# Bilinear sampling as one matmul over all pixels, with weights multiplied out and spread over partitions by DMA, in a new order of the last pass

## The chip, the cores and the metric

The kernel runs on one core of one Trainium2 chip. Its time is the device time of one execution in microseconds (us). The engines are PE (matmuls, with PEld for the loading of weights), DVE, ACT and POOL; SP issues the DMAs. Each runs its own program in order and they meet by semaphores.

## The reference

16 images of 16x16 pixels with 96 channels go through two layers. Layer 0 is a windowed attention and a binarized MLP whose activations are scaled by a maximum over groups of images. Layer 1, the last pass of the kernel, is a deformable attention and a mixture of experts. For every image it computes, in short:

```python
q = x @ w_q + b_q
t = gelu(layernorm(grouped_conv3x3(q)))          # 6 groups of 16 channels
offset = tanh(t_group @ w_offp) * (8, 8)         # one (y, x) per pixel and group
pos = offset + pixel
xs = bilinear_sample_zero(x_group, pos)          # zero outside the image
k, v = xs @ w_k, xs @ w_v
y = softmax(q k^T * scale) v @ w_o               # 12 heads, all 256 pixels
out = top2_of_4_experts(layernorm(x + y)) + ...
```

The bilinear sample of output pixel q in group g is the sum over all pixels (r, c) of hat(y_q - r) * hat(x_q - c) * x[r, c], where hat(d) = max(0, 1 - |d|).

## The kernel before, in words

The kernel has a setup, pass a (layer 0's attention), a short pass b and pass c (layer 1). Pass c is a software pipeline: in turn j, image j is in stage o (offsets), j-1 in s (sample), j-2 in k (split), j-3 in a (attend) and j-4 in e (experts) (BEHIND_C, L79). There are 4 turns that fill it, 12 in the loop and 4 that drain it. The string ORDER_C (L76) is the order of the work: each letter lets every engine run the next step of that stage, so all engines go through the letters in one and the same order, each at its own pace. Below, "o9" is the tenth letter o, and so on. Stages of different images are interleaved in this way and every engine still runs strictly in order: an instruction that waits holds all behind it on its engine.

Stage o: o0 scales the residual (ycl, L846) and SP loads xraw (L427), o1 adds them on DVE (L852, after waiting for xraw) and takes statistics, o2 normalizes (f_xn, L859), then come projection, 3x3 convolution, norm (L865 to L871) and Gelu; o9 is the offset matmul (PE, L1424) and ACT's tanh (L1152), o10 makes hat[group*16+r, axis, q] on DVE (L880 to L882).

How the weights get to the sampling: POOL splits f_xn and the vertical hat into three bf16 parts each (parts, L589 to L595, four operations a time). SP writes these to DRAM (L435, L447) and reads them back in another layout, six DMAs of 48 KB for rows (L444) and six for hatst (L452), so that a contraction over 96 partitions covers 16 rows times six products of parts. PE transposes the horizontal hat (L1429) and ACT copies it (hatx, L1156).

Stage s (L887, L1435) works on six pieces (two tiles of 128 pixels, three pairs of groups). PE contracts over rows (two bf16 matmuls, L1445) into PSUM bank 1, DVE multiplies by the horizontal weights (L896) and sums over columns (L899). One bank serves all pieces, so a piece of PE waits for DVE's multiplication of the piece before (L1443). Then PE transposes xs (L1450), ACT copies (L1166), PE makes keys and values (L1455).

Stage a: 24 transposes on PE (turn, L1470), copies on ACT (L1042), scores and their negated maxima on DVE (L920), then scores again, exponentials on ACT (L1198) and values on PE (L1499; four matmuls of 32 columns side by side, L1495). Stage e: projection, residual and norm (L942), gate, and four experts whose hidden parts share PSUM bank 6 (up L1557, down L1568).

SP is in order too. In each turn it issues the out DMA at e15 (L474), at o12 the reads of rows, the write and the reads of the hats, and at o0 of the next turn the load of xraw, which DVE needs at o1.

## Time and profile before

| | us |
|---|---|
| median of 3 runs | 1477.58 (1475.88 to 1477.93) |
| the profiled execution, its own time | 1476.25 |
| its span, first to last instruction | 1474.5 |
| pass c, first instruction to the end | 445.9 to 1474.5 |
| granted TensorE clock, mean | 0.76 |

Times in the trace count from the start of the span. "Idle before" is how long an engine had stood still before an instruction, and the arrow names what released it. The granted clock is a share of 2.4 GHz, so 0.50 is 1.2 GHz.

### The profile page before, as it was taken

Reading aid. Unit: us, or ns where it says so; the run is one execution under the profiler, and the core shown is the slowest. Engines: PE = TensorE matmul, PEld = TensorE weight load, DVE = VectorE, ACT = ScalarE, POOL = GpSimd, SP = SyncE. Lnnn points to the kernel's source line nnn. Section 1 sums busy time; section 2 is a strip of 40 time slices with the busy share of each in tenths; the row PEclk is TensorE's granted clock in tenths of the full one; section 3 lists DMA queues with packets and bytes.
Section 4 is the critical chain, followed back from the end, with each engine's and each line's share of the span. In section 5 each row is a group of like instructions: output and inputs, shape, how many; then the busy total and the mean of one; then the engine's idle time right before and its main releaser. Section 6 shows DMA issues by size and latency. Waiting matters only on the chain.

```text
span 1474.5 us, 26072 instructions
## 1 busy us (share of the span) xinstructions
PE 976.5 (66%) x8998; PEld 671.1 (46%) x8998; DVE 763.3 (52%) x2165; ACT 597.5 (41%) x1259; POOL 401.3 (27%) x525
## 2 busy tenths in 40 slices
PE   0266667666564434677777877767777878767876
PEld 0154555554343233354464563554544645534454
DVE  1156666555342444476465564564754655645342
ACT  0255556555351011433444425334334444254542
POOL 3377777776001021211111212111111112111000
PEclk9987676767585555787786886887877878878776
DMA  3000000000000100000000000000000000000000
GB/s 96 9 10 11 10 9 11 9 9 7 6 0 16 26 24 22 24 13 22 23 6 25 15 19 25 15 19 25 9 21 25 8 25 15 19 23 4 4 3 3
DMA packets 51853, 24.46 MB, mean 17 GB/s; under 512 B 37977, under 2 KB 49802, under 8 KB 51818
## 3 DMA queue, kind: packets, MB, share of 16 engines
q1 hardware_dynamic: 51818, 24.01, 6.5%
q8 instruction: 20, 0.33, 0.1%
q14 instruction: 15, 0.12, 0.0%
HBM read 16.10 MB, written 7.88 MB: 16 GB/s over the span
## 4 chain that ended last, share of the span: by engine, by line
PE 24%; issue 18%; DVE 11%; ACT 9%; POOL 3%; DMA 1%; DVEq 0%; SPq 0%; ACTq 0%; POOLq 0%
PE ps L1240 20%; ACT stackt L1042 3%; DVE nm L920 3%; DVE xs L899 2%; DVE samp L896 2%; ACT prob L1198 1%; PE ps L1245 1%; ACT L1198 1%; POOL srstd L516 1%; POOL hatr L592 1%; PE ps L1543 1%; DVE th L880 1%; DVE hat L881 1%; ACT th L1152 0%; ACT hb L1224 0%
## 5 line engine op out<-in xcount | busy, mean ns | idle before, releaser
L1042 ACT COPY stackt<-ps 128x768 bf16<-128x768 bf16 x192 | 142.8, 829 | 92.2 <-PE ps L1245 92.1
L1240 PE MATMUL ps<-stackt 53*64 53x64 bf16 (+3 forms) x2304 | 111.3, 247 | 87.5 <-ACT stackt L1042 50.6
L1240 PE MATMUL ps<-b_xnt,we 128*128 128x256 f32 x384 | 143.5, 494 | 2.6 <-ACT hb L1224 2.3
L1224 ACT ACTIVATE hb<-ps 128x512 f32<-128x512 f32 (+1 forms) x128 | 63.1, 493 | 202.3 <-PE ps L1240 202.1
L552 POOL TENSOR_TENSOR rn<-ss,neghalf 128x24 f32<-128x24 f32 x32 | 132.7, 4163 | 42.1 <-DVE ss L749 42.1
L920 DVE TENSOR_REDUCE nm<-ps 128x2 f32<-128x512 f32 x192 | 120.5, 685 | 30.1 <-PE ps L1240 26.9
L1198 ACT ACTIVATE prob<-ps 128x512 f32<-128x512 f32 x192 | 104.2, 594 | 63.9 <-PE ps L1240 63.8
L1240 PEld LDWEIGHTS ps<-stackt 53*64 53x64 bf16 (+3 forms) x2304 | 49.1, 115 | 170.8 <-issue 58.8
L516 POOL TENSOR_TENSOR prstd<-pveps,neghalf 128x2 f32<-128x2 f32 x48 | 42.5, 885 | 309.8 <-DVE pveps L709 302.5
L1240 PEld LDWEIGHTS ps<-we,hb 128*128 128x128 f32 x768 | 110.7, 220 | 26.0 <-ACT hb L1224 20.5
L1240 PE MATMUL ps<-we,hb 128*128 128x96 f32 x768 | 111.8, 303 | 15.8 <-ACT hb L1224 15.8
L1240 PE MATMUL ps<-prob,va 64*32 64x64 f32 (+1 forms) x2304 | 110.4, 366 | 3.9 <-ACT prob L1198 3.9
L896 DVE TENSOR_TENSOR samp<-ps,hatx 128x512 f32<-128x512 f32 x96 | 66.1, 689 | 84.5 <-PE ps L1240 82.1
L1245 PE MATMUL ps<-identb,stack 128*128 128x128 bf16 x1152 | 98.4, 253 | 9.6 <-DVE stack L726 6.0
L899 DVE TENSOR_REDUCE xs<-samp 128x32 f32<-128x512 f32 x96 | 97.6, 1016 | 3.3
L1245 PEld LDWEIGHTS ps<-identb,stack 128*128 128x128 bf16 x1152 | 89.6, 117 | 19.8 <-DVE stack L726 9.7
L1240 PE MATMUL ps<-wconv,qpad 128*128 128x96 f32 x576 | 80.0, 300 | 21.5 <-ACT y1all L1140 21.5
L1240 PE MATMUL ps<-rows,hatst 128*128 128x256 bf16 x192 | 50.1, 356 | 65.8 <-DVE samp L896 45.2
L1240 PEld LDWEIGHTS ps<-b_xnt,we 128*128 128x128 f32 x384 | 81.9, 244 | 17.3 <-ACT hb L1224 6.0
L1240 PEld LDWEIGHTS ps<-wconv,qpad 128*128 128x128 f32 x576 | 77.9, 216 | 24.7 <-ACT qpad L1139 23.9
L516 POOL TENSOR_TENSOR srstd<-sveps,neghalf 128x2 f32<-128x2 f32 x32 | 22.3, 696 | 153.6 <-DVE sveps L709 153.6
L591 POOL CAST hatp<-hat 96x256 bf16<-96x256 f32 x16 | 6.3, 397 | 208.5 <-DVE hat L882 167.8
(229 smaller groups left out, 1676.4 us busy)
## 6 DMA issues: line engine op xcount, KB each, us to landing
rows<-xn_scratch SPq DMA_DIRECT2D x96, 48.0 KB, 1.9
hatst<-hat_scratch SPq DMA_DIRECT2D x96, 48.0 KB, 2.1
xn_scratch<-xnp SPq DMA_DIRECT2D x48, 48.0 KB, 1.8
hat_scratch<-hatp SPq DMA_DIRECT2D x16, 144.0 KB, 1.9
xraw<-x_scratch SPq DMA_DIRECT2D x16, 96.0 KB, 2.0
out<-acc SPq DMA_DIRECT2D x16, 96.0 KB, 1.8
we<-in_we SPq DMA_DIRECT2D x1, 768.0 KB
xin<-in_x SPq DMA_DIRECT2D x16, 48.0 KB, 1.8
```

The source lines that it names most:

```text
L516: g.tensor_tensor(n["rstd"][:], n["veps"][:], neghalf[:, 0:TILES], ALU.pow).then_inc(S(ready), 1)
L552: g.tensor_tensor(rn[:, t].rearrange("p a h -> p (a h)"), ss[:, t, :], neghalf[:, 0:2 * HEADS], ALU.pow).then_inc(S("a_rn"), 1)
L592: own.link(g.tensor_tensor(left, src, part(0), ALU.subtract))
L880: own.link(v.scalar_tensor_tensor(flat(th), flat(th), SIDE / 2.0, flat(posc), ALU.mult, ALU.add))
L896: v.tensor_tensor(samp[:, k % 2], ps[:, 1, :].rearrange("p (a c) -> p a c", c=GC), hx.to_broadcast([P, 2 * SIDE, GC]), ALU.mult).then_inc( ...
L899: ins = v.tensor_reduce(xs[:, t, 2 * GC * b:2 * GC * (b + 1)].rearrange("p (g k) -> p g k", g=2), samp[:, k % 2].rearrange("p (g c) k -> p ...
L920: v.tensor_reduce(nm[:, t, a, 2 * pq:2 * pq + 2], ps[:, score_bank(u // 2) + a, :].rearrange("p (b n) -> p b n", n=TOK), AX.X, ALU.max, ne ...
L1042: return a.copy(stackt[:, x, :, P * t:P * t + P], bank_bf(bank))
L1198: a.activation(prob[:, u % 4].rearrange("p b n -> p (b n)"), ps[:, 4 + u % 2, :], ACT.Exp, scale=float(HD) ** -0.5).then_inc(S("c_exp"), 1)
L1224: a.activation(hb[:, e % 2].rearrange("p m n -> p (m n)")[:, 2 * TOK * k:2 * TOK * k + n_], ps[:, 6, 0:n_], ACT.Gelu).then_inc(S("c_h"), 1)
L1240: return m.matmul(o, l, r, start=start, stop=stop)
L1245: ins = m.transpose(bank_bf(bank)[:, b, :], stack[:, x, t].rearrange("p h c -> p (h c)")[:, P * b:P * b + P], identb[:])
```

## The change

The split in bf16 parts, the DMAs of rows, the transposes of the horizontal hat and of xs, DVE's six multiplications and six sums and PSUM's intermediate result go. Instead the sampling is one contraction over all 256 pixels, with one weight for each pixel and output. hat is written to DRAM in f32 by two DMAs and read back by three: hatx puts the horizontal hat of column p mod 16 on partition p (16 rows of 6144 bytes, repeated 8 times), haty[t] the vertical hat of row 8t + p div 16 (8 rows, each repeated 16 times). These are 768 KB each. DVE multiplies haty by hatx for four of the groups, POOL for two. PE then runs twelve f32 matmuls (two tiles, six groups) with 32 stationary columns from xz, a copy of f_xn by POOL with the other group of a pair left zero; the result is already transposed. ORDER_C is a new string of 54 letters, s has 6 steps instead of 8. In the new order o0 and o1 come first in a turn, before e0; s0 (first multiplications) is the eighth letter; o9 is at the place of the 42nd and o10 at that of the 49th. The matmuls of s stand at s3 and s4.

```diff
-ORDER_C = "eeeoeeosaeaasaseeeoaaeeeaooseoeaokokkeaeassaasooaaoasoao"
+ORDER_C = "ooeeaoeseeaaoeaaeeeoaaeeeoeaoekoeasosseaaoaksaakoaaoos"
...
-        hatx = sb("hatx", [P, TILES, DG, SIDE])
-
-        xnr = sb("xnr", [P, TILES, C])
-        xnp = sb("xnp", [P, 3, TILES, C], BF16)
-        hatr = sb("hatr", [C, TOK])
-        hatp = sb("hatp", [C, 3, TOK], BF16)
-        rows = sb("rows", [P, SIDE, C], BF16)
-        hatst = sb("hatst", [P, DG, TOK], BF16)
-        samp = sb("samp", [P, 2, 2 * SIDE, GC])
-        xs = sb("xs", [P, TILES, C])
+
+        xz = sb("xz", [P, TILES, DG // 2, 2, 2 * GC])
+        haty = sb("haty", [P, TILES, DG, TOK])
+        hatx = sb("hatx", [P, DG, TOK])
...
-        xn_dram = nc.dram_tensor("xn_scratch", [3, TOK, C], BF16).ap()
-        hat_dram = nc.dram_tensor("hat_scratch", [C, 3, TOK], BF16).ap()
+        hat_dram = nc.dram_tensor("hat_scratch", [2, SIDE, DG, TOK], F32).ap()
...
-                w("rows_in", 0)
+                for _ in range(ORDER_C.count("o") - 3):
+                    yield
+                w("hat", 1)
                 settle(sp, "sp")
-                w("xnp", 1)
+                for axis in range(2):
+                    sp.dma_start(hat_dram[axis].rearrange("r g q -> g r q"), hat[:, axis, :]).then_inc(S("c_hat_out"), 16)
+                w("xst", 0)
                 settle(sp, "sp")
-                for k in range(3):
-                    sp.dma_start(xn_dram[k].rearrange("(t p) c -> p t c", p=P), xnp[:, k, :, :]).then_inc(S("c_xn_out"), 16)
-                for _ in range(ORDER_C.count("o") - 3):
-                    yield
-                w("t3", 0)
+                w("hat_out", 32)
                 settle(sp, "sp")
-                w("xn_out", 48)
-                settle(sp, "sp")
-                for slot in range(6):
-                    src = xn_dram[ROW_PARTS[slot]].rearrange("(r c) k -> r c k", c=SIDE)
-                    sp.dma_start(rows[SIDE * slot:SIDE * slot + SIDE, :, :], src).then_inc(S("c_rows_in"), 16)
-                w("hatp", 1)
-                settle(sp, "sp")
-                sp.dma_start(hat_dram, hatp[:, :, :]).then_inc(S("c_hat_out"), 16)
-                w("hat_out", 16)
-                settle(sp, "sp")
-                for slot in range(6):
-                    src = hat_dram[:, HAT_PARTS[slot], :].rearrange("(g r) q -> r g q", r=SIDE)
-                    sp.dma_start(hatst[SIDE * slot:SIDE * slot + SIDE, :, :], src).then_inc(S("c_hat_in"), 16)
+                row = DG * TOK
+                src = bass.AP(hat_dram.tensor, hat_dram.offset + SIDE * row, [[0, SIDE // 2], [row, SIDE], [1, row]])
+                sp.dma_start(hatx[:].rearrange("p g q -> p (g q)"), src).then_inc(S("c_hat_in"), 16)
+                for t in range(TILES):
+                    src = bass.AP(hat_dram.tensor, hat_dram.offset + t * (SIDE // 2) * row, [[row, SIDE // 2], [0, SIDE], [1, row]])
+                    sp.dma_start(haty[:, t].rearrange("p g q -> p (g q)"), src).then_inc(S("c_hat_in"), 16)
...
-            def parts(own, src, left, part, ready):
-
-                own.link(g.tensor_copy(part(0), src))
-                own.link(g.tensor_tensor(left, src, part(0), ALU.subtract))
-                yield
-                own.link(g.tensor_copy(part(1), left))
-                g.tensor_tensor(part(2), left, part(1), ALU.subtract).then_inc(ready, 1)
+            def weights(g_):
+                return haty[:, :, g_, :], hatx[:, g_:g_ + 1, :].to_broadcast([P, TILES, TOK])
...
-                w("xn_out", 0)
-                w("xn", 1)
-                settle(pool, "pool")
-                yield from parts(own, f_xn[:], xnr[:], lambda k: xnp[:, k], S("c_xnp"))
...
-                w("hat_out", 0)
-                w("hat", 1)
+                w("xst", 0)
+                w("xn", 1)
                 settle(pool, "pool")
-                yield from parts(own, hat[:, 0, :], hatr[:], lambda k: hatp[:, k, :], S("c_hatp"))
+                for odd in range(2):
+                    ins = g.tensor_copy(xz[:, :, :, odd, GC * odd:GC * odd + GC],
+                                        f_xn[:].rearrange("p t (b a k) -> p t b a k", a=2, k=GC)[:, :, :, odd, :])
+                ins.then_inc(S("c_xz"), 1)
+                yield
                 yield
 
             def sample_c(i):
-                for _ in range(8):
+                w = waits(pool, "c_", i)
+                w("hat_in", 48)
+                for g_ in (1, 3):
+                    y, x = weights(g_)
+                    g.tensor_tensor(y, y, x, ALU.mult).then_inc(S("c_pmul"), 1)
+                    yield
+                for _ in range(ORDER_C.count("s") - 2):
...
-                w("hatp", 0)
-                w("hxt", 0)
+                w("hat_out", 0)
...
             def sample_c(i):
                 w = waits(dve, "c_", i)
-                own = Own(dve, "dve_sample")
-                for k in range(6):
-                    t, b = k // 3, k % 3
-                    if k == 0:
-                        w("hatx", 1)
-                    w("t3", k + 1)
-                    hx = hatx[:, t, 2 * b:2 * b + 2, :].rearrange("p g c -> p (g c)")
-                    v.tensor_tensor(samp[:, k % 2], ps[:, 1, :].rearrange("p (a c) -> p a c", c=GC),
-                                    hx.to_broadcast([P, 2 * SIDE, GC]), ALU.mult).then_inc(S("c_mul"), 1)
-                    w("mul", k + 1)
-                    ins = v.tensor_reduce(xs[:, t, 2 * GC * b:2 * GC * (b + 1)].rearrange("p (g k) -> p g k", g=2),
-                                          samp[:, k % 2].rearrange("p (g c) k -> p g k c", g=2), AX.X, ALU.add)
-                    if k == 5:
-                        ins.then_inc(S("c_xs"), 1)
-                    else:
-                        own.link(ins)
-                    yield
-                yield
-                yield
+                w("hat_in", 48)
+                for g in (0, 2, 4, 5):
+                    x = hatx[:, g:g + 1, :].to_broadcast([P, TILES, TOK])
+                    v.tensor_tensor(haty[:, :, g, :], haty[:, :, g, :], x, ALU.mult).then_inc(S("c_mul"), 1)
+                    yield
+                for _ in range(ORDER_C.count("s") - 4):
...
-                w("mul", 0)
-                w("hxt", 1)
-                a.copy(hatx[:].rearrange("p t g c -> p (t g c)"), ps[:, 0, 0:2 * C]).then_inc(S("c_hatx"), 1)
...
-                w("hat", 1)
-                for t in range(TILES):
-                    ins = m.transpose(tiles(0, C)[:, t, :], hat[:, 1, cols(t)], ident[0:C, 0:C])
-                ins.then_inc(S("c_hxt"), 1)
...
                 w = waits(pe, "c_", i)
+                yield
+                yield
+                yield
                 w("v", 0)
-                w("rows_in", 96)
-                w("hat_in", 96)
-                for k in range(6):
-                    t, b = k // 3, k % 3
-                    if k >= 1:
-                        w("mul", k)
-                    for g in (2 * b, 2 * b + 1):
-                        ins = mm(ps[:, 1, TOK * (g % 2):TOK * (g % 2) + TOK], hatst[:, g, cols(t)], rows[:, :, GC * g:GC * g + GC])
-                    ins.then_inc(S("c_t3"), 1)
-                    yield
-                w("xs", 1)
-                for t in range(TILES):
-                    ins = m.transpose(ps[0:C, 1, cols(t)], xs[:, t, :], ident[:])
+                w("xz", 1)
+                for odd in range(2):
+                    w("mul", (3, 4)[odd])
+                    if odd:
+                        w("pmul", 2)
+                    settle(pe, "pe")
+                    for t in range(TILES):
+                        for b in range(DG // 2):
+                            ins = mm(ps[32 * b:32 * b + 32, 1, 0:TOK], xz[:, t, b, odd, :], haty[:, t, 2 * b + odd, :],
+                                     t == 0 and odd == 0, t == TILES - 1 and odd == 1)
+                    if odd == 0:
+                        yield
                 ins.then_inc(S("c_xst"), 1)
```

## Rows read from the trace of the kernel before

**Rows 1.** The page, part 1: busy time of each engine, share of the span, instructions.
```profile
PE 976.5 (66%) x8998; PEld 671.1 (46%) x8998; DVE 763.3 (52%) x2165; ACT 597.5 (41%) x1259; POOL 401.3 (27%) x525
```
**Rows 2.** Start of L880 (us, duration) in the first and last of 13 turns, timeline of DVE.
```profile
610.60 0.69 DVE L880 SCALAR_TENSOR_TENSOR th<-th,posc 96x512 f32<-96x512 f32 x1 [4.36 <-ACT th L1152]
...
1306.69 0.69 DVE L880 SCALAR_TENSOR_TENSOR th<-th,posc 96x512 f32<-96x512 f32 x1 [5.35 <-ACT th L1152]
```
**Rows 3.** Windows of a turn: length, busy PE, PEld, DVE, ACT, POOL, clock, DMA, GB/s.
```profile
918.90:955.30 36.40, 27.54 (x204) 19.69 (x204) 24.00 (x53) 13.65 (x30) 6.08 (x12) 0.87 0.06 15
955.30:976.20 20.90, 14.90 (x94) 8.87 (x94) 9.68 (x38) 10.04 (x21) 3.80 (x7) 0.74 0.09 26
```
**Rows 4.** Groups by line and shape in the turn 910.5 to 967.8: busy us, mean ns.
```profile
L899 DVE TENSOR_REDUCE xs<-samp 128x32 f32<-128x512 f32 x6 | 6.1, 1020 | 0.2
L1240 PE MATMUL ps<-prob,va 128*32 128x256 f32 x48 | 5.1, 512 | 0.3 <-ACT prob L1198 0.3
...
L896 DVE TENSOR_TENSOR samp<-ps,hatx 128x512 f32<-128x512 f32 x6 | 4.1, 688 | 4.0 <-PE ps L1240 3.8
...
L1240 PE MATMUL ps<-rows,hatst 128*128 128x256 bf16 x12 | 2.8, 322 | 2.2 <-DVE samp L896 2.2
...
L1450 PE MATMUL ps<-ident,xs 128*96 128x128 f32 x2 | 0.7, 436 | 0.0
```
**Rows 5.** Waits in the same turn: engine and line, releaser, us in total, times, longest.
```profile
PE ps L1240 <- DVE samp L896: 2.2, 2, 1.4
...
PE ps L1394 <- DVE f_xn L714: 1.5, 1, 1.5
...
PE ps L1240 <- ACT y1all L1140: 1.3, 1, 1.3
```
**Rows 6.** Timeline from the offset matmul to the next turn: start us, us, engine, line.
```profile
955.32 2.02 PE L1240 MATMUL ps<-tnt,woffp 128*96 128x256 f32 x4 [0.46 <-ACT tnt L1149]
...
959.55 0.42 DVE L882 TENSOR_SCALAR hat<-hat 96x512 f32<-96x512 f32 x1
...
962.57 0.30 SPq L447 DMA_DIRECT2D hat_scratch<-hatp  x1
...
964.51 2.67 SPq L452 DMA_DIRECT2D hatst<-hat_scratch  x6
...
965.51 0.35 DVE L942 TENSOR_TENSOR xres<-y1all,ps 128x192 f32<-128x192 f32 x1 [1.88 <-PE ps L1240]
...
967.61 0.57 DVE L714 TENSOR_SCALAR b_xn<-xres,smv,srstd 128x96 f32<-128x96 f32 x2 [0.80 <-POOL srstd L516]
...
970.23 2.05 PE L1240 MATMUL ps<-b_xnt,we 128*128 128x256 f32 x4
...
972.03 0.35 DVE L852 TENSOR_TENSOR xin<-xraw,ps 128x192 f32<-128x192 f32 x1 [0.23 <-DVE sc L958]
...
973.69 0.69 POOL L516 TENSOR_TENSOR prstd<-pveps,neghalf 128x2 f32<-128x2 f32 x1 [6.11 <-DVE pveps L709]
```
**Rows 7.** Windows in the setup: large loads in rows of some KB; eight ebraw loads.
```profile
16.00:18.00 2.00, 0.00 (x0) 0.00 (x0) 0.00 (x0) 0.00 (x0) 0.00 (x0) 1.00 0.99 356
...
32.00:33.00 1.00, 0.00 (x0) 0.00 (x0) 0.00 (x0) 0.00 (x0) 0.00 (x0) 1.00 0.63 73
```
**Rows 8.** DMA packets while bt_scratch is written, ebraw is read, hat_scratch is written.
```profile
DMA packets 24, 0.01 MB, mean 8 GB/s; under 512 B 12, under 2 KB 24, under 8 KB 24
...
DMA packets 832, 0.35 MB, mean 55 GB/s; under 512 B 832, under 2 KB 832, under 8 KB 832
...
DMA packets 112, 0.15 MB, mean 134 GB/s; under 512 B 16, under 2 KB 112, under 8 KB 112
```
**Rows 9.** Timeline of DVE, first to second turn: hat done, then xraw used.
```profile
475.25 0.42 DVE L882 TENSOR_SCALAR hat<-hat 96x512 f32<-96x512 f32 x1
...
485.05 0.35 DVE L852 TENSOR_TENSOR xin<-xraw,ps 128x192 f32<-128x192 f32 x1 [8.68 <-DMA xraw<-x_scratch]
```
**Rows 10.** Durations (ns min/median/max) of one DVE line with two inputs in SBUF.
```profile
L871 DVE TENSOR_TENSOR tn<-tn,lnb x16: 357/958/964, 469.1 to 1291.4; 128x192 f32<-128x192 f32 x16
```

More of the change, by code:

```diff
@@ L257, in build_program @@
         gam_ready = [plain_sem(f"gamma_ready{n}") for n in range(2)]
-        own_sems = {k: plain_sem(k) for k in ("dve_first", "dve_mid", "dve_last", "dve_sample", "pool_split", "pool_parts")}
+        own_sems = {k: plain_sem(k) for k in ("dve_first", "dve_mid", "dve_last", "dve_sample", "pool_split")}
         signals("a_", "sp", x_in=48, x1_out=48)
@@ L270, in build_program @@
         signals("b_", "pe", y2=GIMG)
-        signals("c_", "sp", x_in=16, xn_out=48, rows_in=96, hat_out=16, hat_in=96, out=16)
-        signals("c_", "dve", ycl=1, xadd=1, var=1, xn=1, cvar=1, cn=1, hat=1, mul=6, xs=1, nm=12, parts=1,
+        signals("c_", "sp", x_in=16, hat_out=32, hat_in=48, out=16)
+        signals("c_", "dve", ycl=1, xadd=1, var=1, xn=1, cvar=1, cn=1, hat=1, mul=4, nm=12, parts=1,
                 on=2, x3=1, var3=1, xn3=1, gsub=1, acc=2)
-        signals("c_", "pool", rstd=1, xnp=1, crstd=1, hatp=1, va=1, split=1, rstd3=1)
-        signals("c_", "act", xnt=1, qpad=1, q_new=1, cg=1, tnt=1, tanh=1, hatx=1, xst_sb=1, k_sb=1, v=1,
+        signals("c_", "pool", rstd=1, crstd=1, xz=1, pmul=2, va=1, split=1, rstd3=1)
+        signals("c_", "act", xnt=1, qpad=1, q_new=1, cg=1, tnt=1, tanh=1, xst_sb=1, k_sb=1, v=1,
                 copies=1, qt_sb=2, kt_sb=2, q2t_sb=2, exp=12, ot=3, ont=1, x3t_sb=1, gexp=1, h=8)
-        signals("c_", "pe", yt=1, xt=1, qc=1, q=1, conv=1, tt=1, offs=1, hxt=1, t3=6, xst=1, kv=1,
+        signals("c_", "pe", yt=1, xt=1, qc=1, q=1, conv=1, tt=1, offs=1, xst=1, kv=1,
                 qt=2, kt=2, s=12, q2t=2, st=12, pv=12, otr=2, ontp=1, proj=1, x3t=1, gate=1, h1=8, y=2)
@@ L358, in build_program @@
         DSETUP = 28
-        PZERO = 16
+        PZERO = 15
         PSETUP = PZERO + 6
@@ L497, in _ @@
                 setup(g.memset(t[:], 0.0))
-            setup(g.memset(rows[:], 0.0))
-            setup(g.memset(hatst[:], 0.0))
+            setup(g.memset(xz[:], 0.0))
             setup(g.memset(bias3[:], 0.0))
@@ L587, in _ @@
             pool.wait_ge(setup_pool, PSETUP + 1)
-            def parts(own, src, left, part, ready):
-                own.link(g.tensor_copy(part(0), src))
-                own.link(g.tensor_tensor(left, src, part(0), ALU.subtract))
-                yield
-                own.link(g.tensor_copy(part(1), left))
-                g.tensor_tensor(part(2), left, part(1), ALU.subtract).then_inc(ready, 1)
+            def weights(g_):
+                return haty[:, :, g_, :], hatx[:, g_:g_ + 1, :].to_broadcast([P, TILES, TOK])
             def offsets_c(i):
                 w = waits(pool, "c_", i)
-                own = Own(pool, "pool_parts")
                 yield
@@ L1162, in sample_c @@
                 w = waits(act, "c_", i)
-                for _ in range(6):
+                for _ in range(ORDER_C.count("s") - 2):
                     yield
@@ L1384, in offsets_c @@
                 w = waits(pe, "c_", i)
-                w("hatx", 0)
+                w("tanh", 0)
                 w("ycl", 1)
```

4 lines of the change are left out of this document (1 added, 3 removed).

## The prediction

> **What bounds the kernel now.** I read the page first: PE is busy 66% of the span and no engine more [rows 1], so the end is set by chains, not by one engine's work. The change touches pass c alone, so I look at its turn. The offsets' first DVE step (L880) starts at 610.60 and twelve turns later at 1306.69 [rows 2]: 58.0 us a turn. The turn whose timeline I use takes 57.3, and I cut it where PE starts the scores and where it starts the offset matmul. The middle, 36.4 us, has PE busy 27.5 and DVE 24.0 at a clock of 0.87; the wrap around the turn's end, 20.9 us, has PE busy only 14.9 at 0.74 [rows 3]. In the middle PE stands still 8.9 us. The waits of the turn say for whom: 2.2 us for DVE's multiplication of the samples, 1.5 for f_xn, which DVE reaches only after sample work, 1.3 for ACT's copies before the convolution [rows 5]. In the wrap the chain runs offset matmul, tanh, hat (done at 959.97), out and back through DRAM, and beside it projection, norm and gate [rows 6].
>
> **What goes.** DVE loses six pairs of 0.688 and 1.020 us, 10.2 us a turn. PE loses twelve matmuls (2.8) and two transposes of xs (0.7) [rows 4]. Ten of the twelve (2.3) and the transposes stand in the middle. POOL loses eight operations of the split, which no PE instruction waited for directly. SP loses 16 DMAs and keeps 5 beside xraw and out.
>
> **What comes.** Four multiplications of 128x512 f32 on DVE; the old ones, with one input in PSUM, took 0.688 [rows 4], so 2.8 us, and DVE's net is -7.4. With both inputs in SBUF a line can be held up: L871 takes 357 ns alone and 958 in most turns, when POOL works beside it [rows 10]. The bounds for one multiplication are 0.69 and about 1.9 (that ratio); I take 0.7 to 1.2, because only two multiplications of POOL stand beside the four. The nearest row for the twelve new matmuls is prob,va: 48 records, two for each f32 matmul, busy 5.1 us with strips of 32 columns side by side [rows 4], so 0.21 each and 2.6 for twelve. If strips did not overlap, a record's 512 ns would give up to 12 us; three strips instead of four make 3.5. I take 2.6, half of it in the middle, for it is the same shape on the same engine.
>
> The Trainium skill (SBUF — State Buffer, Who interferes with whom) says that a DVE instruction with two SBUF inputs and a GpSimd instruction that reads SBUF exclude each other. By it a multiplication of DVE could wait for a whole one of POOL. The trace agrees in kind (357 against 958 ns).
>
> **The middle, added up.** PE work: 27.5 - 2.3 - 0.7 + 1.3. The new order also moves one of six score and value steps (0.85 of values, with its scores an estimated 1.5) and f_xn's transposes (0.4) to the wrap, and an expert step (estimated 0.6) in. That gives 24.5. Of the 8.9 idle I take off 5.0: no sample wait, f_xn made long before its use, and expert and score steps between ACT's copies and the convolution. The middle becomes 24.5 + 3.9 = 28.4, a gain of 8.0. What is late next there is the pace of scores, exponentials and maxima.
>
> **The wrap, added up.** Here the change adds the wait that I think decides. SP issues three loads of 768 KB and then, in the same queue, xraw of the next image; o1 on DVE waits for xraw, and o1 now stands ahead of e0. Behind it on DVE wait the residual and norm of e1 and f_xn; POOL's power and PE's gate wait for these.
> From the start of the offset matmul: hat is done after 4.65 us (955.32 to 959.97). The store: the second issue starts 0.5 later, and from the issue of the old store to the next DMA's issue 1.94 went by (962.57 to 964.51) [rows 6]; with 0.5 more because the new store's outermost dimension is six groups (see the packets below), 3.0 us. Then 1.3 us until data flow and land, an estimate from the same 1.94. Then 2.36 MB. The full rate in this trace is 356 GB/s at a busy share of 0.99 [rows 7], which gives 6.6 us. But the packet counts tell something else: a store from 12 partitions has 12 packets beside its 12 rows, the eight ebraw loads of 96 rows each have 832 - 768 = 64, eight apiece, and the hat store from 96 partitions has 112 - 96 = 16 [rows 8]. The extra packets follow the outermost dimension, and are at most 16; I read them as one per DMA engine that takes part. Those loads of eight outermost rows moved only 73 GB/s [rows 7]. The three new loads all have eight outermost in their source (8 repeats, or 8 rows), so I expect half the engines: 2.36 MB at 178 GB/s is 13.2 us; eight engines alone may be a little quicker each, and I take 12.5. xraw lands at hat + 3.0 + 1.3 + 12.5 = 16.8. The bounds of this term are 6.6 and, at ebraw's rate, 32.
> After xraw: the addition and statistics, 1.7 (972.03 to 973.69); the residual's norm to b_xn, 2.7 (965.51 to 968.18); then transposes, gate and first expert step, 4.1 (968.18 to 972.28) [rows 6]; less 0.1 that overlaps: 8.4. The wrap is 4.65 + 16.8 + 8.4 = 29.85, against 20.9 before. Of PE's work there, some 14.4 us need no xraw (14.9, less an estimated 3.7 of gate and experts, plus 1.9 and 1.3 that the order puts there), with some 3 of waits for exponentials; then it stands still for some 7 us.
>
> The Trainium skill (DMA: Bandwidth & Descriptors, Why a DMA increments its semaphore by 16 and not by 1) speaks against this change: a DMA from SP uses the largest number of engines up to 16 that divides the slowest dimension of both sides, and the lowest-numbered ones. By it the three loads queue on the same eight engines, one behind the other, and the store runs on six. The packet counts agree with the number; which engines they are, no row here shows.
>
> **The sum.** A loop turn: 28.4 + 29.85 = 58.25, +0.95 against 57.3; twelve make +11.4. In turns 2 and 3 xraw came 9.4 us after hat (475.67 to 485.05) [rows 9] and DVE stood 8.7 for it; now 16.8, so +7.4, less about 3 for sampling that leaves f_xn's way: +4.4 each, and +1.5 for turn 4. Turn 17, without offsets: -3 for the sampling, +3 for late weights. Turns 18 to 20 hold attention and experts alone: 0, the same steps in about the same interleaving. Setup: nothing, one memset less on POOL under the loads. Sum: 1476.25 + 11.4 + 10.3 = 1498.0. The profiled execution is 1.3 below the median of the runs, so no correction is worth making.
>
> **Rivals.** A: all 16 engines take part. The extra packets might count something else, and ebraw's rows are short and badly placed. Then xraw is at hat + 10.9, the wrap 4.65 + 10.9 + 8.4 = 23.95, a turn 52.35: -4.95 x 12 = -59, the first turns -2, turn 17 -4: 1411, faster. It decides at PE's own work in the wrap: as long as xraw comes within 12 to 13 us of hat, the middle's gain of 8 us stays. B: eight engines a load, but not the same eight, so that loads overlap: 8.7 us of data, a turn of 54.5, 1476 - 34 + 1 = 1443. C: a repeated read of the same 6 KB rows is slow. At ebraw's 73 GB/s the data take 32 us, 19.5 more in each of 16 turns: 1810. For it speaks only that no load of before repeats rows; against it, that ebraw's rows are 452 bytes and these 6144. D: the change is neutral because wrap and middle trade exactly; that lies inside the forecast's own error, 1 us a turn being 16 us.
> The forecast itself has +-2 us a turn (DVE's multiplications up to 1.2, strips of PE, idle of 3.9 between 2 and 6), so 1465 to 1535.
>
> **Chances.** Forecast 0.62 (a tenth of it ends faster, a tenth the same), A 0.20, B 0.12, C 0.06. A measurement here tells 0.2% (3 us) from no change. Faster: 0.20 + 0.12 + 0.06 = 0.38; same 0.06; slower 0.56. The range must reach down to A, 1410, and up to the forecast's 1535; left out are C and half of A.
>
> **What would show it.** DMA share in the wrap near 0.5 for 12 us with about 180 GB/s; DVE's L852 idle for 5 to 10 us before it, released by xraw; sixteen or eight extra packets for each of the three loads; the middle down to 28 or 29 us; PE idle for 5 to 8 us before f_xn's transposes, and the clock at 1.2 GHz there. I am wrong if xraw lands less than 13 us after hat, or if the middle stays at 36 us.

## The result, and the profile after

The changed kernel takes 1644.3 us (median of 4 runs, 1639.6 to 1647.5) beside 1477.3 for the kernel before (4 runs): a ratio of 1.113 [1.110, 1.116]. The forecast was 1498, with a range from 1410 to 1535. The direction was right and the size was not.

The page of the changed kernel, parts 1, 4, 5 and 6, in lines that answer to [rows 1] or are new:

```profile
PE 913.2 (56%) x9126; PEld 645.0 (39%) x9126; DVE 673.7 (41%) x2037; ACT 588.9 (36%) x1243; POOL 409.3 (25%) x460
...
issue 52%; PE 18%; POOL 9%; DVE 8%; DMA 6%; ACT 4%; SPq 2%; POOLq 1%; DVEq 0%; ACTq 0%
...
L836 DVE TENSOR_TENSOR xin<-xraw,ps 128x192 f32<-128x192 f32 x16 | 5.7, 354 | 340.4 <-DMA xraw<-x_scratch 340.4
...
L875 DVE TENSOR_TENSOR haty<-haty,hatx 128x512 f32<-128x512 f32 x64 | 65.3, 1058 | 18.2 <-DMA haty<-hat_scratch 18.2
...
xraw<-x_scratch SPq DMA_DIRECT2D x16, 96.0 KB, 21.1
```

PE is 63 us less busy than before, DVE 90, and the span is 163 longer. The one new large number is the third line: DVE's o1, the addition of the residual (L836), stands idle for 340 us in 16 turns, and what ends it is the load of xraw, a transfer of 96 KB that needs 21.1 us from issue to landing. The waits by engine show who stands behind DVE:

```profile
PE ps L1362 <- DVE f_xn L698: 357.5, 16, 30.3
ACT f_xnt L1103 <- PE ps L1362: 352.3, 16, 34.3
DVE xin L836 <- DMA xraw<-x_scratch: 340.4, 16, 27.2
```

One wait passes through three engines. Now the timeline of one loop turn, which answers to [rows 6] (start us, us, engine, line):

```profile
1260.31 1.10 PE L1208 MATMUL ps<-tnt,woffp 128*96 128x256 f32 x4
...
1263.59 0.42 DVE L865 TENSOR_SCALAR hat<-hat 96x512 f32<-96x512 f32 x1
1264.12 1.56 SPq L426 DMA_DIRECT2D hat_scratch<-hat  x2
1268.12 0.61 SPq L433 DMA_DIRECT2D hatx<-hat_scratch  x1
1268.78 1.22 SPq L436 DMA_DIRECT2D haty<-hat_scratch  x2
1270.62 0.41 SPq L418 DMA_DIRECT2D xraw<-x_scratch  x1
1292.03 0.35 DVE L836 TENSOR_TENSOR xin<-xraw,ps 128x192 f32<-128x192 f32 x1 [22.09 <-DMA xraw<-x_scratch]
...
1295.79 0.66 PE L1362 MATMUL ps<-ident,f_xn 128*96 128x128 f32 x2 [22.70 <-DVE f_xn L698]
...
1295.95 1.54 DVE L698 TENSOR_SCALAR b_xn<-xres,smv,srstd 128x96 f32<-128x96 f32 x2 [0.22 <-POOL srstd L499]
1296.17 1.26 POOL L604 TENSOR_TENSOR haty<-haty,hatx 128x512 f32<-128x512 f32 x1
...
1297.55 0.67 PE L1509 MATMUL ps<-ident,b_xn 128*96 128x128 f32 x2 [1.10 <-DVE b_xn L698]
...
1299.55 2.05 PE L1208 MATMUL ps<-b_xnt,we 128*128 128x256 f32 x4
```

SP's queue works first in, first out here: xraw is issued 0.6 us after the last haty and lands behind all 2.36 MB. And the windows of the same turn, with the columns of [rows 3]:

```profile
1260.31:1301.54 41.23, 13.70 (x120) 7.98 (x116) 9.57 (x33) 11.31 (x24) 3.65 (x6) 0.69 0.29 65
1301.54:1329.43 27.89, 25.13 (x193) 18.54 (x192) 18.80 (x50) 12.38 (x28) 6.97 (x9) 0.87 0.01 4
1270.00:1292.00 22.00, 2.63 (x32) 2.20 (x32) 0.00 (x0) 3.27 (x5) 0.00 (x0) 0.63 0.49 109
```

The first window is the wrap, the second the middle. The middle fell from 36.4 to 27.9 us, as the change could hope; the wrap grew from 20.9 to 41.2. In the third window PE and ACT finish what they have (2.63 and 3.27 us busy, all before 1275.2); from there to the landing of xraw only DMA works. The window has half of the 16 DMA engines busy, at 109 GB/s. Over the span, by the start of ACT's tanh: from the first to the fourth, in the fill, 171.9 us against 136.8 before (+35); the 12 turns from there 68.8 us each against 58.0 (+130); from the last tanh to the end 168 in both. That is the 163 us of the spans, the rest lying before the first tanh.

### The profile page after: what moved, and what is told of

Same layout as the page of the kernel before. It is cut to its first block, busy times and chain, and to the rows that moved or that the text cites. A ratio compares the mean times of both kernels' runs of the same rounds, so it can differ in the third digit from the quotient of the medians.

```text
span 1637.8 us, 25699 instructions
## 1 busy us (share of the span) xinstructions
PE 913.2 (56%) x9126; PEld 645.0 (39%) x9126; DVE 673.7 (41%) x2037; ACT 588.9 (36%) x1243; POOL 409.3 (25%) x460
## 3 DMA queue, kind: packets, MB, share of 16 engines
q1 hardware_dynamic: 32938, 50.73, 13.5%
## 4 chain that ended last, share of the span: by engine, by line
issue 52%; PE 18%; POOL 9%; DVE 8%; DMA 6%; ACT 4%; SPq 2%; POOLq 1%; DVEq 0%; ACTq 0%
PE ps L1208 17%; POOL rn L535 3%; DMA xraw<-x_scratch 3%; POOL prstd L499 2%; DVE haty L875 2%; DMA haty<-hat_scratch 1%; POOL haty L604 1%; ACT prob L1166 1%; POOL va L506 1%; SPq L358 1%; POOL srstd L499 1%; DVE tn L698 1%; PE ps L1329 1%; DMA hat_scratch<-hat 1%; ACT sq L1025 1%
## 5 line engine op out<-in xcount | busy, mean ns | idle before, releaser
L1362 PE MATMUL ps<-ident,f_xn 128*96 128x128 f32 x32 | 10.6, 435 | 357.5 <-DVE f_xn L698 357.5
L1208 PE MATMUL ps<-b_xnt,we 128*128 128x256 f32 x384 | 134.3, 466 | 25.9 <-ACT hb L1192 25.7
L836 DVE TENSOR_TENSOR xin<-xraw,ps 128x192 f32<-128x192 f32 x16 | 5.7, 354 | 340.4 <-DMA xraw<-x_scratch 340.4
L891 DVE TENSOR_REDUCE nm<-ps 128x2 f32<-128x512 f32 x192 | 119.2, 683 | 44.8 <-PE ps L1208 43.8
L1103 ACT COPY f_xnt<-ps 96x256 f32<-96x256 f32 x16 | 5.9, 367 | 352.3 <-PE ps L1362 352.3
L1208 PEld LDWEIGHTS ps<-we,hb 128*128 128x128 f32 x768 | 105.5, 212 | 13.1 <-issue 8.8
L1208 PE MATMUL ps<-prob,va 64*32 64x64 f32 (+1 forms) x2304 | 90.5, 327 | 9.2 <-ACT prob L1166 9.2
L1208 PEld LDWEIGHTS ps<-b_xnt,we 128*128 128x128 f32 x384 | 75.0, 225 | 43.9 <-ACT hb L1192 35.4
L1213 PE MATMUL ps<-identb,stack 128*128 128x128 bf16 x1152 | 87.9, 237 | 7.8 <-DVE stack L710 4.5
L1213 PEld LDWEIGHTS ps<-identb,stack 128*128 128x128 bf16 x1152 | 79.0, 108 | 17.8 <-DVE stack L710 8.2
L875 DVE TENSOR_TENSOR haty<-haty,hatx 128x512 f32<-128x512 f32 x64 | 65.3, 1058 | 18.2 <-DMA haty<-hat_scratch 18.2
## 6 DMA issues: line engine op xcount, KB each, us to landing
xraw<-x_scratch SPq DMA_DIRECT2D x16, 96.0 KB, 21.1
```

Of the source, the lines that this page charges most:

```text
L875: v.tensor_tensor(haty[:, :, g, :], haty[:, :, g, :], x, ALU.mult).then_inc(S("c_mul"), 1)
L891: v.tensor_reduce(nm[:, t, a, 2 * pq:2 * pq + 2], ps[:, score_bank(u // 2) + a, :].rearrange("p (b n) -> p b n", n=TOK), AX.X, ALU.max, ne ...
L1208: return m.matmul(o, l, r, start=start, stop=stop)
L1213: ins = m.transpose(bank_bf(bank)[:, b, :], stack[:, x, t].rearrange("p h c -> p (h c)")[:, P * b:P * b + P], identb[:])
```

## The experiments

My theory after the result: the 2.36 MB move far slower than the engines' full rate, and what they cost is the wait of o1 for xraw behind them. Rivals: rows read again and again are slow; the number of engines alone is the cause; or the new order is at fault. Each kernel was run once with a profile, beside the kernel before (1471 to 1476 us), unless a number of runs is given. The kernels that read another tensor, and lanes16, leave out the right sampling weights; they are there for their times alone. A packet time is the median over the packets of 6144 B of the first exchange in the loop's fill, where nothing else runs.

### The transfer: how many engines, and which rows

**distinct8.** The same eight engines, but 128 different rows of another tensor.

```diff
-src = AP(hat_dram, ..., [[0, 8], [row, 16], [1, row]])            # hatx; haty alike
+src = AP(we1, ..., [[row, 8], [row * 8, 16], [1, row]])           # both
```

> The three loads of 768 KB read 128 different rows of 6144 bytes (those of an input of weights) instead of 16 or 8 rows repeated; still eight outermost, same count and size of packets, same destination. The weights of the sampling are other numbers, so the output is another. Theory P (eight engines, and each slowed at the SBUF side because several write neighbouring partitions together): packets stay at 455 ns, 115 GB/s, time 1640 +-10. Theory R (repeated reads of the same rows are slow): packets near 234 to 270 ns, xraw some 10 us earlier a turn, time near 1480.

Measured 1613.5 us; L836 waits 312 us, a packet takes about 400 ns instead of 455, and xraw lands after 19.4 us. Repetition costs at most 31 of 1644 us. The other theory did not come out exactly either: it expected packets to stay at 455 ns.

**lanes16.** The two outer dimensions of each source exchanged, so 16 groups of 8.

```diff
-[[0, 8], [row, 16], [1, row]]     # hatx
+[[row, 16], [0, 8], [1, row]]
-[[row, 8], [0, 16], [1, row]]     # haty
+[[0, 16], [row, 8], [1, row]]
```

> The two outer dimensions of each source are exchanged, so that 16 stand outermost: hatx [16 rows, each 8 times], haty [16 times, 8 rows]. Same rows, same bytes; partition p gets the row of another pixel, so the output is another. Theory R: the same 115 GB/s or so, DMA share near 1 or packets of 900 ns, time 1640. Theory E (only the number of engines matters): 2.36 MB at 350 GB/s or near, xraw at hat + 12 instead of 28, PE's own work ends the wrap, time near 1410 to 1430. Theory P: 16 engines, each with 8 neighbouring partitions, somewhere from 216 to 350 GB/s, time 1410 to 1490.

Measured 1473.9 us, 58.8 us a turn. L836 waits 182 us, xraw lands after 10.5. All 16 engines work, yet a packet takes 444 ns, as slow as with eight. So 230 GB/s, not 356.

**distinct16.** Sixteen groups, different rows.

```diff
+src = AP(we1, ..., [[row, 16], [row * 16, 8], [1, row]])          # both
```

> Like lanes16 (16 outermost, all engines), but the loads read 128 different rows instead of repeated ones; the weights of the sampling are other numbers, so the output is another. So far a packet of 6144 bytes took 455 ns (8 engines, repeated), 400 (8, distinct), 444 (16, repeated), against 234 for the load of weights in the setup. Theory P (what slows each engine is where it writes: the source's three-dimensional form gives each engine a block of neighbouring partitions): 400 to 440 ns, 230 to 260 GB/s, time 1455 to 1475. Theory R (repetition slows at 16 engines): packets near 240 ns, 350 GB/s, time 1425.

Measured 1473.4 us, 439 ns a packet, L836 waits 184 us: repeated rows play no part with 16 engines.

**flat16.** The plain form: row p to partition p.

```diff
+src = we1.rearrange("p e h -> p (e h)")                           # both
```

> The three loads read the weights' array in its plain form, 128 rows onto 128 partitions, as the load in the setup does; same bytes, packets and destination, 16 engines; the sampling's weights are other numbers, so the output is another. Theory P: packets back to about 234 ns and 350 GB/s, because here the engines write partitions apart from each other: xraw at hat + 12.5, time 1420 to 1435. Rival (pass c's own traffic or the row size slows an engine, whatever the form): 400 ns as in the others, time 1455 to 1475.

Measured 1404.5 us, below the 1420 to 1435 expected, 53.8 us a turn, 234 ns a packet, L836 waits 117 us. Here are the windows of the first exchange, first of distinct16 (last columns: clock, DMA share, GB/s):

```profile
482.00:484.00 2.00, 0.00 (x0) 0.00 (x0) 0.00 (x0) 0.00 (x0) 0.00 (x0) 0.50 0.99 221
484.00:486.00 2.00, 0.00 (x0) 0.00 (x0) 0.00 (x0) 0.00 (x0) 0.00 (x0) 0.50 1.02 224
```

The same windows of flat16:

```profile
482.00:484.00 2.00, 0.00 (x0) 0.00 (x0) 0.00 (x0) 0.00 (x0) 0.00 (x0) 0.50 1.02 412
484.00:486.00 2.00, 0.00 (x0) 0.00 (x0) 0.00 (x0) 0.00 (x0) 0.00 (x0) 0.50 0.99 412
```

All 16 engines are busy in both; the bytes differ by 1.85. And of the changed kernel:

```profile
485.00:490.00 5.00, 0.00 (x0) 0.00 (x0) 0.00 (x0) 0.00 (x0) 0.00 (x0) 0.50 0.52 117
```

Half the engines, each at the slow rate of distinct16 and not at that of flat16. Two factors of nearly two stand on top of each other.

### What makes a packet slow

**block16.** flat16's rows and addresses, written as 16 groups of 8.

```diff
+src = AP(we1, ..., [[row * 8, 16], [row, 8], [1, row]])           # both
```

> Each of the three large transfers reads the 128 rows of we1 as flat16 does, row p to partition p, but written as 16 groups of 8 rows instead of 128 rows, so the weights hold other numbers. If the source's addresses made the packets of distinct16 slow (its rows were read in another order), packets take about 235 ns here and the run is flat16's 1404 us. If the form does it (16 groups, each engine with one run of 8 neighbouring partitions), packets take about 440 ns and the run is distinct16's 1473 us.

Measured 1402.2 us and 234 ns. The rule "three dimensions are slow" fell, unless these dimensions are merged into one of 128 on the way, which the trace doesn't tell.

**split16.** Each load becomes eight plain ones of 16 partitions with the right rows, 24 in all.

```diff
+for r in range(8):
+    sp.dma_start(hatx[16 * r:16 * r + 16], AP(hat_dram, 16 * row, [[row, 16], [1, row]]))
+for t in range(2):
+    for r in range(8):
+        sp.dma_start(haty[16 * r:16 * r + 16, t], AP(hat_dram, (8 * t + r) * row, [[0, 16], [1, row]]))
```

> The three transfers are issued as 24 plain ones of 16 partitions each, with the same rows to the same partitions, so each engine should get one partition of each 16. Theory (an engine is slow where it writes a run of neighbouring partitions): packets near 235 ns although haty's source row is the same 16 times. Rival (reading the same row again, or the store's rows just written, slows them): packets stay at 400 ns or more. In both cases the issues bind: SP needed 0.66 us from hatx's issue to haty's, so 24 take about 16 us and xraw lands some 18 to 20 us after the first, not much before the 22 of the changed kernel: 1560 to 1640 us.

Measured 1551.8 us, and 682 ns a packet, for hatx's different rows and for haty's repeated ones alike. My theory of neighbouring partitions for one engine is refuted: here each engine writes partitions 16 apart and is slower than ever. The 24 issues took 11.0 us, not 16. Two explanations were left: neighbouring source rows read at the same time, or partitions written at the same time.

**blockgap16.** block16, its groups 512 bytes nearer in the source, so that nothing can be merged.

```diff
-[[row * 8, 16], [row, 8], [1, row]]
+[[row * 8 - 128, 16], [row, 8], [1, row]]
```

> block16 with the groups 512 bytes nearer each other in the source, so that it cannot be merged into one run of 128 rows; the weights hold other numbers. At any moment 16 engines read rows 48 KB apart. Theory (ways into SBUF: in the order of lanes16, engines 8 partitions apart write at once and two share a way): packets 415 to 465 ns, run about 1473 us, like distinct16. Rival (neighbouring source rows): 234 ns and 1403 us, like block16.

Measured 1479.8 us and 423 ns; in the second half of the exchange, groups of 32 packets alternate between about 405 and 441 ns. Far source rows don't help.

**splitfar16.** split16's 24 loads, with source rows 48 KB apart.

```diff
+src = AP(we1, r * row, [[row * 8, 16], [1, row]])                 # both
```

> split16 with source rows of we1 that lie 48 KB apart (eight rows) in each of the 24 transfers of 16 neighbouring partitions; the weights hold other numbers. Theory (ways into SBUF): packets stay at 680 to 715 ns, the run at about 1550 us. Rival (neighbouring or repeated source rows): packets near 234 ns, the issues (4.0 and 7.7 us by split16's trace) bind and the run is 1450 to 1490 us.

Measured 1558.4 us and 691 ns. Windows of the first exchange, splitfar16:

```profile
480.00:485.00 5.00, 0.00 (x0) 0.00 (x0) 0.00 (x0) 0.00 (x0) 0.00 (x0) 0.50 1.04 144
485.00:490.00 5.00, 0.00 (x0) 0.00 (x0) 0.00 (x0) 0.00 (x0) 0.00 (x0) 0.50 1.02 140
```

The same of split16:

```profile
480.00:485.00 5.00, 0.00 (x0) 0.00 (x0) 0.00 (x0) 0.00 (x0) 0.00 (x0) 0.50 1.06 149
485.00:490.00 5.00, 0.00 (x0) 0.00 (x0) 0.00 (x0) 0.00 (x0) 0.00 (x0) 0.50 1.04 144
```

With 16 engines, changing the source to other rows or to rows far apart changes little in either arrangement (423 to 444 ns, and 682 to 691); with eight engines it took 455 to 400. So repeated, neighbouring or far rows don't explain 234 against 440 or 690 ns, and how the destination partitions are divided over the engines is what is left. That is an argument by exclusion, with two gaps. block16 must be counted as the plain form. And both fast forms read 768 KB that lie in one piece, while no run loads 128 partitions in the plain form from scattered rows; against a source in one piece as the cause speaks only that each of split16's hatx loads reads one piece of 96 KB and is slow. Which partitions meet is inferred too, since the packet records name no engine:

| engines and the partitions that they write at one time, if the outermost dimension is dealt to them in equal runs | packet, ns |
|---|---|
| flat16, block16: plain 128 | 234 |
| lanes16, distinct16, blockgap16: 16 engines, 8 apart | 423 to 444 |
| changed kernel: 8 engines, 16 apart | 455 |
| split16, splitfar16: 16 engines, neighbours | 682 to 691 |

The Trainium skill (SBUF — State Buffer, Door 1: The DMA port swizzle) has a map that fits: 16 ports of 8 partitions, where four neighbours share one with the four that lie 32 further. By it the second and third line put two engines on each port in use and the last one four. The plain transfer has one port per engine (the Trainium skill, DMA: Bandwidth & Descriptors, The descriptor swizzle). An estimate from flat16's 234 ns would be 468 ns with two on a port and 936 with four. The first is 3 to 11% above the 423 to 455 measured, so the traces agree roughly. The second is above the 682 to 691 measured; successive transfers of split16 fall on different ports by that map, so engines that drift apart would meet less, but no run here shows that.

### The wait, and the order

**xraw_act.** The load of xraw from ACT's queue, at o0.

```diff
-sp.dma_start(xraw[...], x1_dram[...]).then_inc(S("c_x_in"), 16)    # SP, turn's start
+act.dma_start(xraw[...], x1_dram[...]).then_inc(S("c_x_in"), 16)   # ACT, o0
```

> ACT issues the load of xraw, so it doesn't queue behind the weights; nothing else changes. My theory (the wait of o1 for xraw holds the projection's norm and f_xn): L836 waits under 3 us, but DVE and POOL now wait at s0 (eighth letter) for the weights, some 12 to 15 us; 4 to 6 us a turn gained, time near 1560. Rival (the weights' lateness alone sets the turn, through s0): no gain, 1630 to 1645.

Measured 1507.5 us, 60.7 a turn: a larger gain than expected, and not in the way expected. L836 still waits 175 us, not under 3 a turn, and xraw takes 13.7 to land instead of 21.1: from another queue it does not get past engines that are full, it only shares them. And a new wait stands behind, DVE's for haty, 109 us.

**old_order.** The changed kernel's sampling with ORDER_C of before (and s on DVE, POOL and PE delayed by two more empty steps).

> The new sampling with ORDER_C of the kernel before (two more empty steps of s in front, so that the first multiplications stand at the third s). o1 now stands behind e0 to e4. Theory (the wrap's wait is the loss, and the old order overlaps the norm, gate and first expert step, 6.8 us, with it): about 6 us a turn gained, time near 1550. Rival (the new order is worth more in the middle than it costs in the wrap): 1640 or more.

Measured 1635.2 us, 67.1 a turn, 272 us of waits for xraw. The expected 6 us a turn did not come, only 1.7, and no run here shows what held the rest. So the new order is not the cause of the loss, but gives nothing either as long as the wait stands.

**early8.** xraw is loaded one turn ahead: after o1's addition SP issues the load of the next image (x1_scratch gets one image more, so that the last turn loads something).

```diff
 # SP, pass c, at o2
+w("xadd", 1)
+sp.dma_start(xraw[:, :, :], x1_dram[i * TOK:(i + 1) * TOK])
```

> The load of xraw for the next image is issued by SP in the same turn, right after o1 has read the buffer, long before the weights' loads; the loads stay as in the changed kernel (eight engines). L836 no longer waits for a DMA. But s0, eighth letter, waits for the weights, which land 28 us after hat: the turn ends about 3.7 + 27.5 + 2 + 28 = 61 us long. Time 1490 to 1530, near the run with xraw on ACT (1507). Rival (xraw was the only wait that matters): 1350 to 1400.

Measured 1523.4 us, 61.9 a turn. The wait for xraw is gone, and most of it has come back elsewhere. Waits of early8:

```profile
DVE haty L877 <- DMA haty<-hat_scratch: 274.0, 16, 23.5
```

340 us for xraw became 274 for haty: s0 stands early in the order, before e0.

**early8_late** puts s0 behind o5, **late8** does that without the early xraw:

```diff
-ORDER_C = "ooeeaoeseeaaoeaaeeeoaaeeeoeaoekoeasosseaaoaksaakoaaoos"
+ORDER_C = "ooeeaoeeeaaoeaaeeeoaaeeeoseaoekoeaosseaaoaksaakoaaoos"
```

> As early8, and the letter s0 (first multiplications on DVE and POOL) moved from the eighth place to behind o5, so nothing waits for the weights in the wrap although they still take 28 us on eight engines. Theory (the loss is two waits for the transfer, and the transfer itself costs nothing once it is covered): no DMA wait above 1 us on DVE and POOL in the loop, turn 49 to 51 us, time 1340 to 1380, below the kernel before. Rival (three f32 multiplications in a row, f32 matmuls or the new order limit the middle): turn above 55 us, time above 1430.

> The changed kernel with one letter moved: s0 from the eighth place to behind o5. The load of xraw stays behind the weights' loads. If o1's wait for xraw is the only wait that sets the wrap in the changed kernel: no change, 1630 to 1645, L836 still waits 21 us a turn. Rival (the first multiplications in the wrap cost something of their own): 10 us or more faster.

Measured: early8_late 1333.1 us, 47.8 a turn; late8 1648.6, the changed kernel's time. Neither wait may be first in line: with both out of the way the transfer, still 115 GB/s, costs little in the loop (perm16_late, below, has it faster and its 12 turns are 7 us shorter). Waits of early8_late:

```profile
POOL haty L606 <- DMA haty<-hat_scratch: 285.3, 16, 23.9
...
DVE haty L877 <- DMA haty<-hat_scratch: 65.4, 8, 23.3
```

POOL's 285 us are harmless as far as the waits show: DVE waits for POOL's normalizing steps no longer than in the changed kernel (f_xn 15.3 against 14.6 us, b_xn 23.6 against 23.3). DVE's 65 are nearly all in the first three exchanges (22.9, 23.3, 13.8 us), in the fill, where no other work covers them.

**old_early.** The old order with xraw early; the first multiplications stand one step later than in old_order, at the fourth s.

> The new sampling in the order of the kernel before (first multiplications at the fourth s), with xraw loaded early, so no DMA wait is left in the loop, as in the fastest run. It divides that run's gain of 139 us between the sampling and the order. If the sampling alone gives it (10 us of DVE a turn gone): 1340 to 1370. If the new order gives part: 1380 to 1430. I expect 1400, because in the old order PE still waits for the norm of e1 behind other work.

Measured 1404.7 us. This parts the change: without the wait for xraw the new sampling gives 70 us in the old order, and the new order, with s0 late, another 72 (1333.1). The load of xraw behind the weights and s0 ahead of them take 311 together (1644.3 - 1333.1): with xraw alone put right 190 are left (early8).

### Faster versions

**perm16_late.** early8_late with lanes16's sources. To keep the sum right, the pixels of a tile lie on the partitions as (c r) instead of (r c): xraw and out move in two DMAs each, the copies of f_xnt and ont read permuted.

> As early8_late, but the pixels of a tile lie on the partitions by column first, so that the loads of the weights have 16 outermost and run on all 16 engines; xraw is loaded and the output stored in two DMAs each, and three copies read or write with a stride. The weights arrive 10 us earlier. Theory (a covered transfer costs nothing): within 10 us of early8_late's 1333. Rival (late weights or DMA traffic still hold something there): 1310 or less.

Measured 1287.7 us, 45 below early8_late, where at most 10 were expected. The first three exchanges of the fill, uncovered, make 31 of it (126.3 against 95.0 us from the first tanh to the fourth; waits for haty 59.9 against 29.7), the loop 7, the drain 10. "Covered" was true of the loop only.

**final.** early8_late with the second s moved forward too.

```diff
-ORDER_C = "ooeeaoeeeaaoeaaeeeoaaeeeoseaoekoeasosseaaoaksaakoaaoos"
+ORDER_C = "ooeeaoeeeaaoeaaeeeoaaeeeosesaoekoeaosseaaoaksaakoaaoos"
```

> As early8_late, with the letter s1 (second multiplications) moved forward to behind e9 as well, so that DVE's multiplications no longer stand three in a row, beside POOL's, ahead of PE's matmuls, where PE waits 1.8 us for them. Theory: 0.5 to 1.5 us a turn, time 1310 to 1327. Rival (the scores' maxima on DVE are then late instead): 1333 or more. Either way more than 9% under the kernel before.

Measured 1305.2 us (5 runs), ratio to before 0.885 [0.884, 0.887]; 45.3 us a turn, 2.5 less than early8_late where 0.5 to 1.5 was expected.

**split16_final** and **perm16_final**: final with split16's loads, and with perm16_late's pixels.

> split16's transfers in the version of the label final (xraw early, sampling late). If packets are fast, the last haty lands about 17 to 19 us after the first issue instead of 22 to 24, so the waits of the three filling turns (60 us in all) shrink by about 4 us each and the loop keeps its 45.3 us a turn: 1285 to 1305 us, against 1305. If SP, now busy some 16 us longer with issues at o1, delays the load of xraw at o2, then nothing is lost, since that load has a turn of slack.

> perm16_late with the order of final. Between perm16_late and early8_late the trace puts 31 of the 45 us in the first three turns after the fill (126.3 us against 95.0 from the first tanh to the fourth, waits for haty 59.9 against 29.7), where nothing covers the exchange, and 7 in the loop and 10 in the drain. If that is the cause, it adds to final's gain of 2.5 us a turn in the loop: final's 1305 less 31 to 45, 1260 to 1274 us. If the gain of the pixel order lay in the loop's cover, final's tighter loop would change it and the sum is off by over 10 us.

Measured 1250.8 us (4 runs), 0.850 [0.847, 0.854], and 1251.3 us (4 runs), 0.850 [0.847, 0.853]: 15% below the kernel before and 24% below the changed one, and not to be told apart. Both came out below what was expected. They come to the same time by different ways: the fill, first tanh to fourth, takes 111.9 us in split16_final and 96.5 in perm16_final, the twelve turns 512.4 and 525.1. In split16_final a turn is 42.7 us instead of final's 45.3, and the timeline shows a part of it. A turn of final:

```profile
901.95 2.94 POOL L606 TENSOR_TENSOR haty<-haty,hatx 128x512 f32<-128x512 f32 x2 [16.49 <-DMA haty<-hat_scratch]
902.25 3.19 DVE L877 TENSOR_TENSOR haty<-haty,hatx 128x512 f32<-128x512 f32 x2
```

A turn of split16_final:

```profile
864.45 2.49 POOL L608 TENSOR_TENSOR haty<-haty,hatx 128x512 f32<-128x512 f32 x2 [10.69 <-DMA haty<-hat_scratch]
870.49 1.29 DVE L879 TENSOR_TENSOR haty<-haty,hatx 128x512 f32<-128x512 f32 x2
```

The weights land some 6 us earlier against the tanh, POOL has done its half before DVE comes to its own, and DVE's two take 1.29 us instead of 3.19. This turn of final is one of the worse: over its twelve turns the two take 2.0 to 3.5 us, 2.6 on average, in split16_final always 1.29. That is 1.3 of the 2.6 us a turn, if it is all on DVE's path, which no run isolates. The granted clock also rose, from 0.93 to 0.96 over the twelve turns. The page of perm16_final, parts 1 and 4:

```profile
PE 866.9 (70%) x9126; PEld 615.7 (50%) x9126; DVE 671.4 (54%) x2037; ACT 590.2 (47%) x1243; POOL 404.6 (33%) x460
...
issue 27%; PE 20%; DMA 19%; POOL 12%; DVE 11%; ACT 6%; SPq 4%; POOLq 0%; DVEq 0%; ACTq 0%
```

"issue" is down from 52% to 27% of the chain, and PE does the same 9126 matmuls in 46 us less, its clock being granted at 0.84 on average instead of 0.75.

## Why the prediction was right and wrong

The turn from 1260.31 to 1329.43 takes 69.1 us; 58.25 were forecast. Term by term:

| term | forecast | measured |
|---|---|---|
| offset matmul to hat done | 4.65 | 3.70 |
| hat done to the first load's issue (store and back) | 3.0 | 4.1 |
| from there to the use of xraw | 1.3 + 12.5 | 23.9 |
| use of xraw to the first score matmul | 8.4 | 9.5 |
| middle | 28.4 | 27.9 |

**The step that failed** is the third: "2.36 MB at 178 GB/s is 13.2 us; eight engines alone may be a little quicker each, and I take 12.5". The number of engines was right, the rate of one was not: 356 GB/s by 16 engines was taken as 22 GB/s for any engine in any transfer. Measured were 111 to 119 GB/s at a DMA share of 0.49 to 0.52, 13.5 GB/s an engine (6144 B in 455 ns), and 2.36 MB take about 21 us. This one term is 10.1 of the 10.9 us by which the turn missed; over 12 turns 121, and the fill's 35 instead of 10 are the same error in three uncovered exchanges. The row that should have raised the price was there: ebraw's eight rows at 73 GB/s [rows 7], laid to the short rows of 452 bytes. It was kept as an upper bound of 32 us, but only inside rival C with 0.06, and the range left it out.

**Engines.** Right. The extra packets between the first hat and the use of xraw in the fill are 52: 6 + 6 for the two stores, 8 for each of the three loads, 16 for xraw. A share near 0.50 over the whole 20 us says that the three loads queue on the same eight, which was open. The Trainium skill (DMA: Bandwidth & Descriptors, Why a DMA increments its semaphore by 16 and not by 1), cited for this in the forecast, agrees in both. Rival B (other eight, overlapping) is out.

**Rival A** (16 engines, 1411 us) is out for the kernel as changed. Its arithmetic can be tested with the kernels above: with 16 engines at the full rate (flat16) 1404.5 us, within 7 of its 1411. That it is so near is luck in part: the twelve turns gained 50 us where the sum had 59, and fill and drain 21 where it had 6. With 16 engines at the slow rate (lanes16) it is 1473.9. So the number of engines and the rate of each decide between 1404 and 1644.

**Rival C** (repeated rows) is out as a mechanism: different rows on eight engines cost 1613.5, and on 16 nothing changes. Its 1810 us lie 166 above the measured time, the forecast's 1498 lie 146 below it.

**The middle and DVE.** Right: 27.9 us against 28.4, clock 0.87 in both. The first multiplication of this turn, after POOL's, took 0.68 us; the three in the middle took 0.99, 1.75 (beside POOL's) and 1.03, on average 1.26, a little above the upper end of what was taken. The mean is 1.06 over 64.

**After xraw.** 9.5 us instead of 8.4. Nearly 1 us of it is the normalization of b_xn, 1.54 us where it had taken 0.57 [rows 6]: its second half now runs beside POOL's multiplication and takes 1.30 us in each of the twelve turns, against 0.33 in every turn before. The forecast looked at POOL beside DVE's multiplications only.

**PE in the wrap.** A standstill of some 7 us before f_xn's transposes was forecast and 22.7 measured: 11 more come from store and data, and the rest from PE, which had finished what needs no xraw 12.8 us after the offset matmul, not 17.4 (14.4 and 3 of waits). That cost nothing, because xraw was later still. The sign named for the clock came: 0.50 from 1276 to 1291.

**The store.** 4.1 us instead of 3.0. The old exchange wrote from 96 partitions with 16 engines, the new one from six groups; half a microsecond for that was too little. It may be a smaller miss of the same kind as the large one; no run changes the store alone.

## What to carry to other kernels

Price a DMA by a row with the same arrangement of partitions, not by the best rate in the trace: count the groups of the outermost dimension (engines) and ask which partitions these engines write at the same moment; here that was worth a factor of 3.6 in bandwidth, 412 against 115 GB/s. A small load behind a large one in a queue costs what the large one costs, so ask of each transfer who waits for it first in line, and put that consumer where other work stands before it; check the fill and drain apart, since nothing covers there. When a wait is removed, look for the next one on the same transfer before judging (340 us for xraw became 274 for haty, and both gone gave 311 us).

## What the runs showed of the hardware that was not expected

- An engine's packet of 6144 B takes 234, about 440 or about 690 ns on 16 engines, depending on how the load is laid out, with DMA shares near 1.0 in all three; repeated, neighbouring or far source rows don't explain it. A busy share of DMA says nothing of the rate.
- Loads of 16 neighbouring partitions are the slowest per packet (144 GB/s), yet split16_final is as fast as perm16_final: slower by 15 us in the fill, faster by 13 in the twelve turns. Its 24 issues go out at 0.46 us each, and it needs no new pixel order. Why its turn is shorter, 42.7 us against 43.8, no run shows.
- DVE's multiplication with two SBUF inputs takes 0.69 us alone and 1.51 and 1.75 beside POOL's (two in 1.29 against 3.19 us), while POOL's two take 2.49 and 2.94. b_xn's second half, which reads one tensor, is held up too: 1.30 us beside POOL's multiplication, 0.33 alone.
- From the issue of the hat store out of six groups to the next issue, which waits for it, 4.0 us go by for 2 x 96 KB (1264.12 to 1268.12).
